# A small gather of 128 pieces of x ahead of the table's gathers

## The reference

```python
x = x + (x @ weight.T + bias + (x @ A0[id0].T) @ B0[id0].T)   # layer 0: 32 adapters
x = x + (x @ B1[id1].T) @ A1[id1].T                            # layer 1: 8 adapters
```

## Time and profile before

| | us |
|---|---|
| median of 3 runs | 97.74 |
| lowest, highest | 97.5, 97.92 |
| the profiled execution | 97.93 |
| its span, first to last instruction | 96.2 |

### The profile page before, as it was taken

The page is one execution under the profiler, slowest core; times in us unless marked ns, Lnnn a source line. Parts: engine busy times, 40 slices in busy tenths (PEclk is TensorE's granted clock), DMA queues, the critical chain, the costliest instruction groups (busy, mean ns, idle before and its releaser), DMA issues.

```text
span 96.2 us, 2295 instructions
## 1 busy us (share of the span) xinstructions
PE 91.4 (95%) x652; PEld 89.6 (93%) x652; DVE 64.3 (67%) x121; ACT 60.9 (63%) x192; POOL 57.9 (60%) x126
## 2 busy tenths in 40 slices
PE   5999999999998999999999999999999999999980
PEld 5799999999896989999999999999999999999970
DVE  4759997609016757866786777768595867775470
ACT  3244599945729986948686767668486868671210
POOL 6504067800478999999288675949585766808500
PEclk9999999999999999999999999999999999999999
DMA  0999999967576258999999999993826354520206
GB/s 23 310 360 396 410 346 312 237 136 186 145 188 239 53 203 224 257 243 273 227 212 287 286 231 194 227 286 137 237 34 228 31 215 53 200 109 0 109 0 218
DMA packets 16143, 19.38 MB, mean 202 GB/s; under 512 B 1252, under 2 KB 11364, under 8 KB 15972
## 3 DMA queue, kind: packets, MB, share of 16 engines
q1 hardware_dynamic: 14848, 13.97, 51.0%
q0 software_dynamic: 1280, 5.28, 21.7%
q10 hardware_dynamic: 4, 0.00, 0.0%
HBM read 13.40 MB, written 5.84 MB: 200 GB/s over the span
## 4 chain that ended last, share of the span: by engine, by line
PE 85%; POOL 4%; DMA 3%; issue 3%; DVE 1%; DVEq 0%; POOLq 0%; ACT 0%
PE psum L400 51%; PE psum L437 11%; PE psum L385 5%; PE psum L429 4%; PE psum L483 4%; DMA by_rank<-row_ends 3%; POOL gathered_rows L329 3%; PE psum L369 3%; PE psum L377 3%; PE psum L462 2%; PE psum L411 2%; PE psum L445 1%; DVE y L692 1%; POOL g_sel L339 1%; PE psum L492 1%
## 5 line engine op out<-in xcount | busy, mean ns | idle before, releaser
L400 PE MATMUL psum<-wd,xt 128*128 128x256 f32 (+1 forms) x384 | 62.3, 311 | 0.4 <-ACT wd L563 0.2
L400 PEld LDWEIGHTS psum<-wd,xt 128*128 128x128 f32 x384 | 56.2, 188 | 1.0 <-issue 0.9
L563 ACT ACTIVATE wd<-table_rounded 128x128 fp32r x128 | 27.8, 298 | 11.1 <-PE psum L400 9.8
L346 POOL TENSOR_TENSOR up_rows<-gathered_rows,up_rows 128x512 fp32r<-128x512 f32 x16 | 20.6, 1289 | 13.9 <-ACT up_rows L563 13.9
L329 POOL DMA_INDIRECT gathered_rows<-by_rank,rows x16 | 15.9, 993 | 8.5 <-DMA by_rank<-row_ends 5.9
L653 DVE TENSOR_TENSOR xt<-psum,xt 128x512 fp32r<-128x512 f32 x16 | 11.1, 691 | 7.0 <-ACT xt L563 7.0
L660 DVE STREAM_TRANSPOSE psum<-x_squares 128x512 f32<-128x512 f32 x13 | 14.5, 1113 | 1.1 <-issue 1.0
L437 PE MATMUL psum<-up_rows,u_sel 128*128 128x256 f32 x96 | 14.1, 283 | 0.0
L563 ACT ACTIVATE xt<-psum 128x512 fp32r<-128x512 f32 x16 | 9.6, 597 | 7.0 <-DVE psum L660 5.5
L437 PEld LDWEIGHTS psum<-up_rows,u_sel 128*128 128x128 f32 x96 | 12.9, 190 | 0.0
L339 POOL TENSOR_TENSOR g_sel<-gathered_rows,batch_mask 128x16 f32<-128x16 f32 x64 | 12.1, 225 | 0.8 <-DMA gathered_rows<-by_rank,rows 0.5
(11 more groups left out here) (63 smaller groups left out, 67.0 us busy)
## 6 DMA issues: line engine op xcount, KB each, us to landing
out<-y SPq DMA_DIRECT2D x15, 256.0 KB
x_squares<-in_x SPq DMA_DIRECT2D x8, 256.0 KB
w_rows<-in_L_cond_base_weight SPq DMA_DIRECT2D x4, 256.0 KB, 4.7
bw_rows<-in_L_cond_lora_B_w SPq DMA_DIRECT2D x1, 1024.0 KB, 7.2
a_rows<-in_L_cond_lora_A_w SPq DMA_DIRECT2D x1, 1024.0 KB, 10.2
by_rank<-bw_by_rank SPq DMA_DIRECT2D x4, 256.0 KB
x_rows<-in_x SPq DMA_DIRECT2D x3, 256.0 KB, 7.4
x_squares<-in_x SPq DMA_DIRECT2D x12, 64.0 KB, 2.4
```

Source lines behind the costliest of these rows:

```text
L346: nc.gpsimd.tensor_tensor(out=up_rows[:, k % 2, LO, :], in0=gathered_rows[:, k % GATHERS, 0:D], in1=up_rows[:, k % 2, HI, :], op=ALU.subtr ...
L400: last = nc.tensor.matmul(bank_of(k, half)[:, start:end], xt[:, k % X_SLOTS, c, x_part, :], wd[:, w_part, c, col:col + end - start], start ...
L563: return nc.scalar.activation(dst, src, ACT.Copy)
```

## The change

A tile of 128 x 16 floats is added, `trial_rows`, and a semaphore. As soon as `rows` is written, GpSimd issues an indirect DMA that takes 128 pieces of 16 floats (64 bytes) out of x, at the row numbers of block 0. It waits for it before it waits for the table. Nothing reads the tile. All else stays, the table's gathers too.

```diff
+        trial_rows = sb("trial_rows", [P, R])
         gathered_rows = sb("gathered_rows", [P, GATHERS, ROW])
...
+        trial_gathered = sem("trial_gathered")
         table_stored = sem("table_stored")
...
             pool.wait_ge(rows_ready, 1)
+
+            nc.gpsimd.indirect_dma_start(out=trial_rows[:, :], out_offset=None,
+                                         in_=x.rearrange("b s (e r) -> (b s e) r", r=R),
+                                         in_offset=bass.IndirectOffsetOnAxis(ap=rows[:, 0:1], axis=0),
+                                         ).then_inc(trial_gathered, 16)
             pool.wait_ge(ids_in, 32)
             pool.wait_ge(masks_ready, 4)
+            pool.wait_ge(trial_gathered, 16)
             pool.wait_ge(table_stored, (2 * C + 3) * 16)
             gather(0)
             gather(1)
```

## The result

The changed kernel takes 98.34 us (median of 20 runs, 97.91 to 99.47), the kernel before 97.72 (20 runs): a ratio of 1.0067, 95% interval 1.0045 to 1.0089. It is slower, by more than the forecast of no change allows, and just above the range. Now and then an execution of any version is slow as a whole; the ratios leave those out and the medians count them, so a ratio is not quite the quotient of two medians. The profiled execution took 98.15 us, its span 96.4.

What follows compares the result with a forecast made beforehand. TensorE, busy 95% of the span, was taken as the bound. Added issue 0, added wait 0, store +0.1 and first use -0.74, of which TensorE sees 0, left 97.93 us; from the median 97.74, 97.7 was predicted, range 97.3 to 98.3.

Steps and rivals of the forecast that it cites:

- the added issue: GpSimd's issue of the added gather, from 19.25 to 21.21 us, hidden beside the wait for the table: 0; uncovered 1.96 us.
- the added wait: GpSimd's wait for the added gather, landing at 24.0 us, 2.8 behind its issue, before 24.27: 0, margin 0.3 us.
- the packets: The added gather's 128 packets among the table's make the last store of row_ends land 0 to 0.42 us later; taken 0.1.
- the first use: The first table gather, now second of its kind, loses 0.53 us of issue and 0.21 of its run, together 0.74.
- from 30 us on the blocks follow each other at TensorE's own pace: Steady blocks on TensorE: 4.41 us each, with no wait in the list.
- the four rivals: Four other outcomes: 97.4 us (chance 0.13), 97.97 (0.13), 98.7 (0.12) and 97.1 (0.07); the forecast had 0.55.
- C: Slower side: the added gather lands late, at 25.9 us, and holds the table's gathers; end 0.92 later, 98.7; chance 0.12.
- My sign for being wrong: The end moves though base(2) starts within 0.1 us of 30.65, or the chain of waits goes through the added gather.
- the argument that waiting for a DMA does not by itself cost this time: Behind the gather's landing at 29.07 us g_sel works at 29.27, so waiting alone does not cost the 0.80 of issue.
- an earlier gather is worth nothing: Block 0's gathers and g_sel come 0.64 us sooner; TensorE's 0.30 us idle only moves behind the small product; gain 0.

Runs made afterwards that it cites:

- tile_only: The kernel before plus the unused 64-byte tile where the change put it, without the small gather; 98.21 us, ratio 1.0066.
- tile_behind_xt: The whole change, but with the added tile declared behind xt, so that gathered_rows and xt keep their places; 97.63 us, ratio 1.0025.
- after_again: The changed kernel measured once more, unaltered, on one chip with a version that has the tile ahead of wd; 98.41 us, ratio 1.0099.
- gathered_moved: The kernel before, no small gather, with the 64-byte tile rows declared behind gathered_rows, so gathered_rows alone moves; one run, 4.407 us a block.
- shift_512: The kernel before, no small gather, plus an unused tile of 512 bytes a partition ahead of gathered_rows; 97.96 us, ratio 1.0022.
- gather_tile_last: The whole change, but with the added tile declared behind y, the last tile, so that no other tile moves; 97.83 us, ratio 0.9991.
- gather_tile_128: The whole change, but with the added tile 128 bytes a partition instead of 64, the gather filling its first 64; 98.13 us, ratio 1.0044.
- shift_256: The kernel before, no small gather, plus an unused tile of 256 bytes a partition ahead of gathered_rows; one run, 4.407 us a block.

## Why the prediction was wrong

**The step that failed** is one that was not taken. The sum had the added issue, the added wait, the packets and the first use; the added tile had no term, and "from 30 us on the blocks follow each other at TensorE's own pace" was taken as a constant. The pace depends on where `wd` and `xt` stand to each other, and the tile is declared between them: +0.046 us a block, 0.46 us in the ten blocks read above. tile_only pays the whole 0.66% and has no gather. From block 1 to the last it is 0.53 us. The 0.1 us that the medians lose beyond that I could not place in single profiles, whose starts scatter by 1 us. None of the four rivals held it either. C had the sign and, at 98.7, a size near it, by another mechanism, which did not occur. My sign for being wrong, an end that moves though `base(2)` does not, came in a sharper form: `base(2)` started 0.29 us sooner and the end came later.

**Right: the issue and the wait are hidden.** The issue was over at 20.55, not 21.21: even the first indirect DMA had only 0.29 us ahead of it. The landing came 2.2 us behind the end of the issue; I had taken 2.8 from the 330 KB gather. The Trainium skill (DMA: Bandwidth & Descriptors, Anatomy of one DMA) with its fixed 2.0 us was nearer here. But it is no constant: from the start of the instruction, which takes 1.16 us, the seven profiles with a small gather have 3.4, 3.5, 3.9, 4.1, 4.2, 4.3 and 4.7 us. Less the 1.16 us that is 2.2 to 3.5, and in five of the seven nearer 2.8 than 2.0. In tile_behind_xt the landing came at 19.09 + 4.3 = 23.4, still ahead of the table at 23.92, and in after_again, the latest, at 18.92 + 4.7 = 23.6, ahead of 23.89. The 0.1 us for its packets can't be told from nothing: `row_ends` took 3.38 and 3.65 us to land in these two, and 3.13 to 3.86 in the five profiles without a small gather whose chain shows it.

**Half right: what the first use costs.** The first table gather took 0.95 us in every kernel with a small gather ahead of it and 1.15 or 1.16 in those without; these 0.21 us are a first use. The 0.80 us of issue are not. The chain of waits of tile_behind_xt, whose small gather went first:

```profile
23.95 0.04 POOLq L360
23.99 0.73 issue
24.71 3.79 DMA gathered_rows<-by_rank,rows
```

The 0.74 us that I took were 0.21 + 0.07. So the argument that waiting for a DMA does not by itself cost this time, taken from `g_sel`, did not carry over to a gather. What the 0.73 us consist of stays open. Of the 0.85 us by which the first gather starts sooner only the 0.07 are of this. The rest is the spread of the moment at which the table has landed: tile_only, without any small gather, starts its first gather at 24.30.

**Right in this profile, not in every one: an earlier gather is worth nothing.** The idle time of TensorE moved from before the small product to behind it, and `base(2)` waited 0.5 us for ScalarE's copies:

```profile
29.32 0.89 ACT L571 ACTIVATE wd<-table_rounded 128x128 fp32r x4
29.47 0.39 PE L437 MATMUL psum<-u_own,g_sel 128*128 128x128 f32 x2
30.33 1.51 PEld L408 LDWEIGHTS psum<-wd,xt 128*128 128x128 f32 x9 [0.66 <-issue]
30.36 1.80 PE L408 MATMUL psum<-wd,xt 128*128 128x384 f32 x9 [0.50 <-ACT wd L571]
```

ScalarE ends at 30.21. These are all engines in order of time in the changed kernel, to be read beside the earlier trace rows. `base(2)` is 0.29 us earlier than there, mostly since ScalarE was: its copies begin at 27.98 instead of 28.19, released by TensorE.

That the small gather did away with the wait for `g_sel` is not shown. tile_only, which has no small gather, has no such wait either, and after_again, which has one, waits 0.35 us. What counts is how long before ScalarE's first copy for block 2 the table lands, and that differs from run to run: 24.27 and 28.19 us in the kernel before, 23.99 and 27.54 in gathered_moved. Nor is an earlier gather always worthless. From that copy to `base(2)` it is 2.46 us in the kernel before and 2.38 in the changed one, but 2.89 in gathered_moved and 2.95 in shift_512, whose waits for `g_sel` are longer. What TensorE waited for in gathered_moved:

```profile
PE psum L429 <- POOL g_sel L339: 0.7, 1, 0.7
PE psum L400 <- ACT wd L563: 0.2, 1, 0.2
```

In such an execution part of the 0.28 us could arrive; no run here shows it.

**What two profiles could not decide.** Theory O, that the sooner gathers set the engines into another rhythm, fitted the two profiles as well as the tile did. Only tile_only, which has one part and not the other, told them apart.

## What to carry to other kernels

A new tile is never only a tile: it moves all that is declared behind it, so in a kernel bound by TensorE declare trial tiles last, or compare against a kernel that has the tile and not the work. When a steady loop changes its pace by about one per cent and no wait does, look at the distance between the two operands' tiles before looking at queues. A wait on a short list that names one engine can hide a second one right behind it, and the order of time shows it.

## What the runs showed of the hardware

**The distance between a product's two operands.** With the distance from `wd` to `xt` at 128 more than a multiple of 256 bytes, 24 products and the rest of a block took 4.407 us; at 160, 192, 0, 64 and 96 they took 4.450 to 4.460. TensorE's granted clock was 1.00 from 42 to 84 us in all eighteen profiles, and moving both tiles together changed nothing. That the weight load of the next product and the moving reads of the present one get in each other's way would explain it, but was only argued; no run separates it from the writes of ScalarE and VectorE to the same two tiles. The Trainium skill (SBUF — State Buffer, Who interferes with whom) gives TensorE two independent read ports, one for the moving operand and one for the weight load; the paces show that in this kernel the time of such products depends on where their two operands stand to each other, and leave open whether the ports are the reason. The products by `u_sel` and `up_rows`, in groups of six, took 0.71 or 0.72 us outside the late blocks below, but they are no test: by the sizes of the tiles the two stand 9,728 bytes apart, 38 x 256, in every kernel here. What another remainder would do to them was not tried.

**A late load of x.** In three of seven profiles with the small gather (gather_tile_last, gather_tile_128, after_again) one block lasts 0.6 to 1.2 us longer, and VectorE waits up to 2.0 us for a load of `x_squares` just before. Chain of waits of after_again:

```profile
38.76 7.11 DMA x_squares<-in_x
45.87 0.03 issue
45.90 0.02 DVEq L667
```

No block is longer in the eleven profiles without the small gather. The late load itself is in two of them, though: VectorE waits 0.6 us for it in tile_only, and in shift_256 (waits, total, times, longest)

```profile
DVE psum L661 <- DMA x_squares<-in_x: 1.3, 2, 0.9
```

without TensorE standing. With the small gather VectorE waits for such a load, 1.1 us or more in all, in five profiles of seven. So the load can be late without the gather. Whether the gather makes it more frequent or later stays open; the medians above don't show a price.
